# A fused Mamba and Hadamard-FFN block on one core: five of sixteen input-projection matmuls change their place in TensorE's order at the head of each round

## The reference

```
# branch 1: selective state-space layer (d_inner 1024, 16 states, dt_rank 128, conv of 4 taps)
proj = layernorm(x) @ W_in + b_in
hidden, gate = split(proj, 2)
conv_out = silu(causal_depthwise_conv(hidden, conv_w, conv_b))
dt_in, Bm, Cm = split(conv_out @ W_x, [128, 144])
delta = softplus(dt_in @ W_dt + b_dt)
A = -exp(a_log)
# per token t:  h = exp(delta_t * A) * h + (delta_t * x_t) * B_t ;  y_t = sum over the 16 states of h * C_t
y = (y + conv_out * d_param) * silu(gate)
x = x + layernorm(y @ W_out + b_out)
# branch 2: gated FFN (inner 2048) between Walsh-Hadamard transforms
z = fwht(layernorm(x) * SU_ug) / 64
z = silu(z @ W_gate.T * scale_gate) * (z @ W_up.T * scale_up)
z = fwht(z * SU_dp) / 64 @ W_down.T * scale_down
x = x + layernorm(z)
```

## Time and profile before

| | us |
|---|---|
| median of 3 runs | 2718.33 (2713.88 to 2719.03) |
| the profiled execution | 2718.33 |
| its span in the trace | 2716.5 |
| TensorE busy | 2580.2 (95%) |
| VectorE busy | 2243.9 (83%) |
| GpSimd busy | 2058.8 (76%) |
| ScalarE busy | 1822.3 (67%) |

### The profile page before, as it was taken

One profiled execution on the slowest core, in us unless ns is written; L12 is line 12 of the kernel. 1 busy time (PEld: TensorE's weight loads), 2 busy tenths in 40 slices (PEclk: granted clock), 3 DMA queues, 4 the chain that ended last, 5 costly groups with the idle time before them and its releaser, 6 DMA issues.

```text
span 2716.5 us, 46264 instructions
## 1 busy us (share of the span) xinstructions
PE 2580.2 (95%) x16016; PEld 2187.0 (81%) x16016; DVE 2243.9 (83%) x2569; ACT 1822.3 (67%) x3944; POOL 2058.8 (76%) x1698
## 2 busy tenths in 40 slices
PE   8698989999999999999999999999999999989986
PEld 6466568888888888889888888889888888878776
DVE  7897888898888888898888888898888888889221
ACT  4676677777777777777777777677777777655221
POOL 6776769788787979888787979888787979766221
PEclk9899999999999999999999999999999999999999
DMA  5554145666666666666666666666666666556686
GB/s 177 208 199 163 67 166 204 228 206 226 217 218 223 216 214 210 229 209 226 215 220 225 214 216 212 223 207 230 217 223 218 220 209 211 201 183 225 225 308 241
DMA packets 166921, 573.85 MB, mean 211 GB/s; under 512 B 17440, under 2 KB 19872, under 8 KB 133920
## 3 DMA queue, kind: packets, MB, share of 16 engines
q1 hardware_dynamic: 166688, 570.88, 61.2%
HBM read 536.74 MB, written 34.08 MB: 210 GB/s over the span
## 4 chain that ended last, share of the span: by engine, by line
PE 72%; DVE 11%; ACT 6%; issue 4%; DMA 3%; POOL 0%; POOLq 0%; DVEq 0%; ACTq 0%; SPq 0%
PE pF L648 21%; PE hT L558 13%; PE pM L576 12%; PE pD L661 9%; PE pM L628 8%; DVE h L1070 5%; DVE acc L1083 4%; PE pM L598 2%; PE pD L681 2%; DMA wug<-scratch_ug 2%; ACT decay L889 1%; PE decay L648 1%; PE hT L550 1%; ACT delta L871 1%; ACT L889 1%
## 5 line engine op out<-in xcount | busy, mean ns | idle before, releaser
L1070 DVE TENSOR_TENSOR_SCAN h<-decay,dbx 128x512 f32<-128x512 f32 x1024 | 1202.1, 1206 | 101.3 <-ACT decay L889 87.9
L1236 POOL TENSOR_TENSOR dbx<-u,bb 128x2048 f32<-128x2048 f32 (+1 forms) x272 | 1177.0, 4328 | 37.6 <-DVE h L1070 35.9
L889 ACT ACTIVATE decay<-delta,a_neg 128x255 f32<-128x255 f32 x2048 | 877.1, 468 | 340.4 <-DVE h L1070 334.2
L648 PE MATMUL pF<-fxT_hi,wug 128*128 128x256 f32 x3840 | 752.0, 289 | 6.5 <-DMA wug<-scratch_ug 4.3
L1083 DVE SCALAR_TENSOR_TENSOR acc<-hT,bcT,acc 128x1024 f32<-128x1024 f32 x480 | 609.8, 1270 | 138.6 <-PE hT L558 135.3
L648 PEld LDWEIGHTS pF<-fxT_hi,wug 128*128 128x128 f32 x3840 | 617.8, 192 | 9.6 <-DMA wug<-scratch_ug 7.0
L558 PEld LDWEIGHTS hT<-ident,h 128*128 128x128 f32 x4096 | 472.7, 141 | 176.7 <-issue 121.1
L558 PE MATMUL hT<-ident,h 128*128 128x128 f32 x4096 | 537.4, 274 | 55.4 <-DVE acc L1083 42.8
L648 PE MATMUL pF<-fxT_lo,wug 128*128 128x256 f32 x1920 | 544.4, 284 | 0.0
L576 PE MATMUL pM<-xnT,w_in 128*128 128x256 f32 x2016 | 483.8, 383 | 13.3 <-ACT hid L814 4.3
L1299 POOL TENSOR_TENSOR prod_lo<-prod,prod_hi 128x256 fp32r<-128x256 f32 x256 | 187.2, 731 | 316.2 <-ACT prod_hi L920 315.7
(11 more groups left out here) (154 smaller groups left out, 2626.4 us busy)
## 6 DMA issues: line engine op xcount, KB each, us to landing
wug<-scratch_ug SPq DMA_DIRECT2D x256, 1024.0 KB, 4.8
wd<-scratch_wd SPq DMA_DIRECT2D x256, 512.0 KB, 4.0
w_in<-in_W_in SPq DMA_DIRECT2D x252, 256.0 KB, 2.9
bb<-scratch_bc SPq DMA_DIRECT2D x128, 256.0 KB, 4.6
xb<-in_hidden_states SPq DMA_DIRECT2D x16, 512.0 KB, 5.0
xr<-in_hidden_states SPq DMA_DIRECT2D x16, 512.0 KB, 5.7
out<-xr SPq DMA_DIRECT2D x16, 512.0 KB, 3.9
had_down<-in_W_down SPq DMA_DIRECT2D x2, 2048.0 KB, 12.3
```

The costliest lines, as they stand in the source:

```text
L648: mm = pe.matmul(gate_up_bank(no)[:, which, :], wug[no % 2][:, 2 * which + a, kt, :], fxT[b][:, kt, :], start=(kt == 0 and i == 0), stop=( ...
L889: e = act.activation(da[q % 2][:, i, 1:], delta[c % 2][:, dt, 1:], ACT.Exp, scale=a_neg[:, dt, n:n + 1])
L1070: dve.tensor_tensor_scan(row(h[n % 2][:, tiles, :]), row(da[q % 2][:, :, :]), row(dbx[n % 2][:, tiles, :]), 0.0, ALU.mult, ALU.add).then_i ...
L1236: pool.tensor_tensor(dbx[n % 2][:, tiles, :], u[:, tiles, :], rows, ALU.mult).then_inc(done if restarts(c) else prod_done, 1)
```

## The change

Two entries of the table and two calls differ. The 8 steps of the hidden half's pair 0, which were all in slot 1 (5 before `turn_h` of the second half, 3 behind it), are now 2 at the end of slot 0, ahead of `turn_f`, and 6 in slot 1 between `turn_f` and `turn_h`. Nothing stands behind `turn_h` in slot 1 any more. Of pair 1 the first 2 steps (not 3) are in slot 2 and 6 (not 5) in slot 3. No instruction is added or removed; only TensorE's order changes.

```
-        PE_HID = {0: (0, range(0, 5)), 1: (0, range(5, 8)), 2: (1, range(0, 3)), 3: (1, range(3, 8)),
+        PE_HID = {0: (0, range(0, 2)), 1: (0, range(2, 8)), 2: (1, range(0, 2)), 3: (1, range(2, 8)),
...
                     if fold is not None:
                         up_gate(fold, HT - 1)
+                    if front is not None:
+                        in_proj("hid", front, *PE_HID[0])
                     return
                 if k == 1:
                     if ff is not None:
                         turn_f(ff)
                     if front is not None:
-                        in_proj("hid", front, *PE_HID[0])
+                        in_proj("hid", front, *PE_HID[1])
                     if back is not None:
                         turn_h(back, NST - 1, 1)
-                    if front is not None:
-                        in_proj("hid", front, *PE_HID[1])
                     return
```

## The result

| | before | after |
|---|---|---|
| median | 2716.15 us (4 runs, 2713.88 to 2719.03) | 2740.95 us (4 runs, 2739.14 to 2745.38) |
| the profiled execution | 2718.33 | 2735.64 |
| its span | 2716.5 | 2733.8 |

The ratio after/before is 1.0086, with a 95% interval of 1.0066 to 1.0105: the change makes the kernel about 0.9% slower, 18 to 29 us, where 20.5 were forecast.

A forecast was written before the change was run, and what follows sets the result against it. TensorE, busy 150.34 of 152.42 us a round, was taken to set the pace. 12 full rounds at 1.67 (20.0) and 0.5 made 20.5 on top of 2718.3: forecast 2739 us, range 2730 to 2754.

The forecast's parts named there:

- TensorE's list sets the round: Full rounds 3 to 14: what lengthens TensorE's list in one by a microsecond lengthens the program by about 12.
- The distance from turn_h to turn_y: Slot 1: with no steps between, the two transpositions start 2.50 us apart, since VectorE must first read `hT`.
- T + 4.35 and T + 6.85: Slot 1: forecast starts of `turn_h` and `turn_y` in us, counted from the moment `up_gate` of `fold` is through.
- The price of 1.24: Slot 1: `turn_y` comes 1.24 us later in a full round than before.
- The sixth step of pair 1: Behind the second `turn_y`: one more step to do there, so 3.09 us becomes 3.52, a loss of 0.43.
- The two steps ahead of turn_f: End of slot 0: they fill no gap and push `turn_f` back by 0.87 us.
- the wait of `turn_h` for `f_low`: Slot 1: over at T + 3.86, before `turn_h` starts at T + 4.35, so it costs nothing.
- Given back late in the round: Rival at 810.30 and after: shorter waits return the loss; 2729 us if half, 2719 if all; chance 0.10.
- The clock: Rival behind `turn_y`: TensorE's clock falls too; 2755 us if in all 12 rounds; chance 0.12 for half or more.
- The rule of the Trainium skill: Slot 1's new stretch: transposes do not count as busy for the clock's gate, so it is one long pause.
- The drop in the earlier trace: Round 1: after a 3.24 us stretch, matmuls ran at a granted clock of 0.58 over 3.20 us, losing 1.34.
- Rounds 0 to 2: Round 0: 0.5 us, within 0 to 1.67; round 1: 0, at most 1.67; round 2: 0, between -1.7 and +0.8.

The follow-up runs named there:

- The statistics experiment: Kernel before with VectorE's second-layernorm statistics moved from slot 25 to the head of slot 29, GpSimd's four operations to slot 30; 2694.72 us, 0.9917 times before.
- it with the statistics late: Changed kernel with VectorE's second-layernorm statistics moved to the head of slot 29; 2717.81 us, 1.0004 times the kernel before.
- pair 0 alone: Changed kernel with pair 1 as before (3 steps in slot 2, 5 in slot 3); 153.65 us a round, 1.0052 times the kernel before.
- pair 1 only: Kernel before with 2 steps of pair 1 in slot 2 and 6 in slot 3; 152.85 us a round, 1.0026 times the kernel before.

## Why the prediction was right

**TensorE's list sets the round.** Right. The order changed by five matmuls, no work was added, and every full round grew by what TensorE idles more. The statistics experiment shows it from the other side: the waits of TensorE in slots 26 and 30 became shorter by 1.29 and 0.13, and the round by 1.44.

**The distance from turn_h to turn_y.** Right, and this is the mechanism. It was taken from the one place in the trace of before where two transpositions were already neighbours, 2.50; after, it is 2.51 in round 4. T + 4.35 and T + 6.85 were forecast for `turn_h` and `turn_y`; measured are 698.90 - 694.57 = 4.33 and 701.41 - 694.57 = 6.84. The stretch from `turn_f` to the second `turn_h` of state 0 is 711.12 - 695.43 = 15.69, as forecast. The price of 1.24 was 1.23 alone.

**The sixth step of pair 1.** Right: 0.43 forecast, 0.43 measured alone. Sum 1.67 forecast, 1.66 measured in one round and in twelve.

**The two steps ahead of turn_f.** The statement that they fill no gap is right in sign, but which part of the change costs was only settled by the runs. With six steps behind `turn_f` its delay costs nothing; with three it costs the whole 0.87. The prediction computed the wait of `turn_h` for `f_low` (over at T + 3.86, before T + 4.35) and so had this right too, without saying that the kernel before sits exactly on that distance.

**Given back late in the round.** The rival is out. The wait ahead of `turn_h` of slot 26 is unchanged (row below): VectorE followed TensorE, as its idle time at 799.74 had said.

```profile
815.08 1.07 PE L558 MATMUL hT<-ident,h 128*128 128x128 f32 x8 [1.13 <-DVE acc L1083]
```

**The clock.** The rival is out for the full rounds. Behind the stretch of two transpositions and 1.47 of wait the granted clock is 1.00, in round 4 and in round 14 as well:

```profile
702.30:705.10 2.80, 2.80 (x26) 2.80 (x25) 2.80 (x6) 0.87 (x2) 2.24 (x1) 1.00 0.70 242
...
2243.10:2246.00 2.90, 2.90 (x27) 2.90 (x26) 2.90 (x6) 0.87 (x2) 2.46 (x2) 1.00 0.71 229
```

In all 13 rounds with this pattern (2 to 14) `up_gate` behind it took 2.95 or 2.96 us, its length at full clock. The rule of the Trainium skill that was weighed (TensorE: Matmul & The Clock Gate, Part 4: PE-mode transpose) would have spoken for a drop; these rows do not show one. They do not refute the rule either, since no run separated transpositions from pure idling.

The drop in the earlier trace rows that spoke for the rival was partly chance. The same two matmuls (L628) behind the same transposition took 1.57 us there, 1.65 in the changed kernel, 2.08 in it with the statistics late, and 1.12 or 1.13 in the other six profiles. The wait ahead of them was 2.20 in the kernel before, where the clock fell, and 2.27 to 2.46 in four of the six where it did not.

**Rounds 0 to 2.** Forecast were 0.5, 0 and 0. By the starts of `turn_x` (224.63 and 381.56 before, 226.06 and 383.84 after) and T of round 3, the three rounds changed by +1.43, +0.85 and -0.81, in sum 1.47. That the sum is small and near the forecast is luck; little of it is the change.

Round 0: the kernel with the statistics late has the order of the kernel before here, since its move needs a `back`, and its `turn_x` starts at 226.27, 1.64 later than in the profile of before. In none of the other eight profiles does it start before 225.83. So the +1.43 is no evidence of a cost.

Round 1: from `turn_x` to the first `turn_y` it is 0.42 longer in the changed kernel (10.91 and 11.33), and 0.41 with pair 0 alone, so the two steps do cost something where 0 was taken. The other 0.43 arises at the stretch of the earlier trace rows, where the clock fell in both.

Round 2: the two steps fill part of `turn_f`'s wait, and the clock does not fall:

```profile
387.01 1.03 PE L576 MATMUL pM<-xnT,w_in 128*128 128x256 f32 x4
388.64 1.07 PE L540 MATMUL hT<-ident,ob 128*128 128x128 f32 x8 [0.60 <-DVE acc L1083]
389.55 2.76 PE L576 MATMUL pM<-xnT,w_in 128*128 128x256 f32 x12
```

The six steps take 2.76 where five took 3.64 before. But that slow stretch does not belong to the old order as such. With pair 1 only, the head of slot 1 is that of before, and its five steps ran at a granted clock of 1.00:

```profile
385.71 1.06 PE L540 MATMUL hT<-ident,ob 128*128 128x128 f32 x8 [1.47 <-DVE acc L1083]
386.61 2.32 PE L576 MATMUL pM<-xnT,w_in 128*128 128x256 f32 x10
```

The clock fell here in three of the five profiles with nothing ahead of `turn_f`, and in none of the four with two steps ahead. Nine executions do not settle whether the two steps prevent it. Against the profile with pair 1 only, where the clock held, `turn_x` to the first `turn_y` is 0.36 longer in the changed kernel (10.80 and 10.44); the prediction had worked out 0.37 for this.

**The total.** The forecast was 20.5 us over the profiled execution. The profiled pair gives 21.44 up to round 15 and 17.3 over the whole span, the medians are 24.8 apart, and the ratio says 18 to 29. The 12 rounds (20.0 forecast and measured) are what was understood. That the forecast of 2739 came within 2 us of the median of 2740.95 is partly luck, since executions of one kernel differ by more than that.

## What to carry to other kernels

When one buffer passes between two engines (here `hT`, written by TensorE and read by VectorE), the distance between two writes is set by write plus read plus hand-over, 2.4 to 2.6 us here, and whatever other work the writing engine has must be laid under these distances. Work moved out of one to a place without a wait costs its length (0.43 for the one step of pair 1; 1.23 for three steps of together 1.31), even where the engine is 95% busy and the total work is unchanged. Read such distances from start to start and compare them with the sum of what stands between; the difference is wait, even where the trace shows little or none of it as idle. And look for an engine's side jobs that stand in the path while the same engine idles a few slots later: moving 1.6 us of them was worth 1.44 us a round, more than any split of the matmuls that was tried.

## What the runs showed that was not expected

The full rounds are repeatable to 0.02 us within a profile, while whole executions of one kernel differ by several. The 13 executions of the changed kernel on record have spans from 2729.5 us (granted clock 0.992) to 2743.5 us (0.987). A share of 0.8% and of 1.3% of the span is 21.8 and 35.7 us; the difference of 13.9 is that of the spans, 14.0. These are the two ends; in between the clock does not say everything: two executions at 0.991 have spans of 2733.8 and 2738.3. So most of the spread between executions goes with the time that TensorE's clock was down, and a part stays open. In the profiles of all nine kernels the window from 400 to 2360 us has a granted clock of 1.00 and their full rounds are alike, so there it arises at the start and in the rounds without a `front`. An effect of a few microseconds is better read from the length of a round than from two medians.
